# Banded attention in eight larger units: four row groups of score matmuls instead of two, one set of score banks, late projections in banks 6 and 7

## The reference

```python
q = (x @ Wq.T).reshape(b, t, h, e) / scale
kk = (xp @ Wk.T).reshape(b, tp, h, e) / scale      # xp: 31 zero rows ahead of x
v = (xp @ Wv.T).reshape(b, tp, h, e)
idx = jnp.arange(t)[:, None] + jnp.arange(k)[None, :]
dot = jnp.einsum('bthe,btkhe->bthk', q, kk[:, idx])
out = jnp.einsum('bthk,btkhe->bthe', softmax(dot), v[:, idx])
return out.reshape(b, t, h * e) @ Wu.T + bu
```

## Time and profile before

| | us |
|---|---|
| median of 3 runs | 705.16 |
| runs | 700.53 to 710.09 |
| the profiled execution, its own time | 708.41 |
| its span | 706.8 |
| banded attention in it, first warming matmul to end of the last output | 398.6 to 507.5 |

### The profile page before, as it was taken

How to read it: one execution, slowest core, us unless ns; L and a number is a source line. 1 busy time by engine, 2 the same in 40 slices (tenths; PEclk the granted TensorE clock), 3 DMA queues, 4 the chain that set the end, 5 groups by cost and what they waited for, 6 DMA issues and landing times.

```text
span 706.8 us, 8340 instructions
## 1 busy us (share of the span) xinstructions
PE 460.1 (65%) x2996; PEld 244.9 (35%) x3018; DVE 498.6 (71%) x675; ACT 202.4 (29%) x234; POOL 351.3 (50%) x309
## 2 busy tenths in 40 slices
PE   6754845166676667668678878999679953544650
PEld 2531313022222222223223446766446622431210
DVE  1947985889999999999973266677345458976421
ACT  2553791033333323333314332111110052102110
POOL 6617217879999999999960034555730000000000
PEclk8857976569999999999999999687769986757775
DMA  7430020645554545555500000000000000000000
GB/s 273 83 166 1 8 75 2 149 118 151 151 150 149 149 149 149 149 149 149 149 1 8 4 1 2 1 2 3 10 9 1 1 0 0 1 1 7 5 4 32
DMA packets 29262, 46.13 MB, mean 65 GB/s; under 512 B 17878, under 2 KB 19320, under 8 KB 28184
## 3 DMA queue, kind: packets, MB, share of 16 engines
q1 hardware_dynamic: 26776, 45.10, 22.2%
q0 software_dynamic: 2368, 0.37, 0.4%
q10 hardware_dynamic: 64, 0.00, 0.0%
HBM read 43.55 MB, written 1.11 MB: 63 GB/s over the span
## 4 chain that ended last, share of the span: by engine, by line
POOL 30%; PE 21%; DVE 20%; issue 18%; SPq 4%; ACT 4%; DMA 2%; DVEq 1%; POOLq 0%; ACTq 0%
POOL dBu L871 13%; POOL hit L858 9%; SPq L650 3%; PE ps L2185 2%; POOL work L918 2%; PE ps L1867 2%; PE ps L2174 2%; POOL work L920 2%; POOL work L907 2%; PE ps L2077 2%; DMA work<-in_L_attn_edge_index 1%; POOL hst L620 1%; PE ps L2107 1%; PE ps L2321 1%; PE ps L1921 1%
## 5 line engine op out<-in xcount | busy, mean ns | idle before, releaser
L2005 PE MATMUL ps<-hC,ident 128*128 128x512 f32 x256 | 121.4, 596 | 0.0
L1089 ACT ACTIVATE ps<-work,a_neg 128x1020 f32<-128x1020 f32 x64 | 71.3, 1115 | 164.5 <-DVE hst L1429 98.8
L1429 DVE TENSOR_TENSOR_SCAN hst<-ps,dBu 128x1024 f32<-128x1024 f32 x43 | 98.2, 2287 | 4.1 <-ACT ps L1089 1.3
L1989 PE MATMUL ps<-late,pick_state 96*128 96x512 bf16 x128 | 39.5, 391 | 84.2 <-DVE hC L1447 67.9
L871 POOL TENSOR_TENSOR dBu<-work,dA 128x1024 f32<-128x1024 f32 x32 | 75.6, 2361 | 2.8 <-DVE hst L1429 2.2
L871 POOL TENSOR_TENSOR dBu<-work,b_sb 128x1024 f32<-128x1024 f32 x32 | 75.9, 2373 | 0.6
L858 POOL DMA_INDIRECT hit<-in_L_attn_edge_values,tab_i x64 | 63.3, 990 | 12.8 <-issue 10.2
L2005 PEld LDWEIGHTS ps<-hC,ident 128*128 128x128 f32 x256 | 49.1, 192 | 43.1 <-issue 34.1
L1989 PEld LDWEIGHTS ps<-late,pick_state 96*128 96x128 bf16 x128 | 7.8, 97 | 135.2 <-DVE hC L1447 116.9
L1802 PE MATMUL ps<-idle_bf,zero_bf 128*128 128x512 bf16 x133 | 39.4, 431 | 20.2 <-issue 16.5
L1447 DVE TENSOR_TENSOR hC<-hst,ps 128x1024 f32<-128x1024 f32 x43 | 51.4, 1196 | 0.8 <-PE ps L1989 0.8
(11 more groups left out here) (358 smaller groups left out, 876.7 us busy)
## 6 DMA issues: line engine op xcount, KB each, us to landing
b_sb<-b_rows_all SPq DMA_DIRECT2D x64, 256.0 KB, 4.1
dA<-b_rows_all SPq DMA_DIRECT2D x64, 256.0 KB, 4.2
work<-in_L_attn_edge_index SPq DMA_DIRECT2D x6, 1024.0 KB, 6.2
dA<-in_L_attn_edge_index SPq DMA_DIRECT2D x1, 1024.0 KB, 10.6
dBu<-in_L_attn_edge_index SPq DMA_DIRECT2D x1, 1024.0 KB, 12.6
hit<-in_L_attn_edge_values,tab_i POOLq DMA_INDIRECT x64, 3.9
late<-work SPq DMA_DIRECT2D x12, 64.0 KB, 2.0
X<-in_x SPq DMA_DIRECT2D x1, 512.0 KB, 3.9
```

Of the source, the lines that this page charges most:

```text
L1089: nc.scalar.activation(dst[:, :, 1:], src[:, :, 1:], ACT.Exp, scale=a_neg[:, n:n + 1]).then_inc(dA_sb, 1)
L1429: V.tensor_tensor_scan(h_buf[i % 3], dA_ps[k], dBu[:, k, :], 0.0, ALU.mult, ALU.add).then_inc(scan_done, 1)
L1989: last = T.matmul(bank(2 + h), pick_state[:, n, :, :].rearrange("p v i -> p (v i)"), parts[:, j * NT + h * HALF:j * NT + (h + 1) * HALF], ...
L2005: last = T.matmul(bank(6 + h), ident[:, :], hC[:, i % 2, h * HALF:(h + 1) * HALF], start=False, stop=(n == S - 1))
```

## The change

The 16 units become 8: a unit is four heads and one block `j` of all four groups, so every instruction of VectorE, ScalarE and GpSimd in steps 2 to 5 handles 1,024 elements a partition instead of 512, and its buffers grow to match. `unit_scores` has 32 matmuls round four row groups, into banks 0 to 3, one for each group. There is one set of score banks, so it waits for the merge of unit u-1. The warming is one matmul for each of the four banks. `unit_values` and `window_values` come twice in a unit, for groups 0, 1 and 2, 3, through the same banks 4 and 5; the first pair's transpositions stand between the merge and the maximum. `unit_output` goes round four column groups. Projections 3 to 7 use banks 6 and 7; 4 to 7 stand in units 0 and 1, two each, every one waiting for the copy of the one before. The clearing of banks 6 and 7 moves to unit 2. ScalarE's copy of the next unit's scores moves behind the exponential.

In the rows below `[waits ...]` names the semaphores of an instruction. First TensorE in the middle of the loop, one unit of before: the scores of a unit (L2107), values (L2121), the output of an earlier unit (L2134).

The diff, cut where it only changes sizes:

```diff
-        s2_buf = [work[:, 8 * NT + k * HALF:8 * NT + (k + 1) * HALF] for k in range(3)]
+        s2_buf = [area(8 + k, 1) for k in range(3)]
...
+        UNITS = 2 * J
+        SEGS = G * WT
...
-        QM_BANK = (0, 2, 4, 0) + (4,) * 4
+        QM_BANK = (0, 2, 4, 6) + (6,) * 4
...
             def window_keys(u):
...
                 nc.scalar.activation(s2_buf[u % 3].rearrange("p (s k) -> p s k", k=C),
-                                     bank(2 * (u % 2), 2).rearrange("p (s w k) -> p s w k", w=2, k=C)[:, :, 1, :],
+                                     bank(0, 4).rearrange("p (s w k) -> p s w k", w=2, k=C)[:, :, 1, :],
                                      ACT.Copy).then_inc(s2_copied, 1)
...
-            for u in range(16):
-                if u < 15:
-                    window_keys(u + 1)
+            for u in range(UNITS):
+                if u < 2:
+                    query_heads(4 + 2 * u)
                 act.wait_ge(s2_shifted, u + 1)
                 nc.scalar.activation(s2_buf[u % 3], s2_buf[u % 3], ACT.Exp).then_inc(s2_exp, 1)
-                if u < 4:
-                    query_heads(4 + u)
+                if u < UNITS - 1:
+                    window_keys(u + 1)
+                if u < 2:
+                    query_heads(5 + 2 * u)
...
-            def window_values(u):
-                dve.wait_ge(v2_ps, u + 1)
-                if u >= 4:
+            def window_values(u, pair):
+                dve.wait_ge(v2_ps, 2 * u + pair + 1)
+                if u >= 4 and pair == 0:
                     dve.wait_ge(o2_ps, u - 3)
...
-            for u in range(18):
-                if u < 16:
-                    window_scores(u)
-                if 1 <= u < 17:
+            for u in range(UNITS + 2):
+                if u < UNITS:
+                    window_merge(u)
+                    window_values(u, 0)
+                    window_shift(u)
+                if 1 <= u <= UNITS:
                     window_sums(u - 1)
                 if u >= 2:
                     window_probs(u - 2)
-                if u < 16:
-                    window_values(u)
+                if u < UNITS:
+                    window_values(u, 1)
...
-            for h in range(3):
+            for h in range(4):
                 project(h)
-            pe.wait_ge(qm_sb, 1)
-            project(3)
...
             def unit_scores(u):
-                hg, j, gp = unit(u)
-                if u < 2:
+                hg, j = unit(u)
+                if u == 0:
                     pe.wait_ge(qm_sb, 4)
                 else:
-                    pe.wait_ge(s2_read, u - 1)
...
-                for d in range(2):
-                    keep_warm(2, 2 * (u % 2) + d)
+                    pe.wait_ge(s2_read, u)
+                for g in range(G):
+                    keep_warm(1, g)
                 for m in range(WT):
-                    for d in range(2):
-                        g = 2 * gp + d
+                    for g in range(G):
                         r = slice(C * g, C * g + C)
-                        last = T.matmul(bank(2 * (u % 2) + d)[:, 2 * C * m:2 * C * m + 2 * C],
+                        last = T.matmul(bank(g)[:, 2 * C * m:2 * C * m + 2 * C],
...
             unit_scores(0)
-            unit_values(0)
-            for u in range(16):
-                if u < 15:
+            unit_values(0, 0)
+            for u in range(UNITS):
+                if u < 2:
+                    pe.wait_ge(qm_sb, 4 + 2 * u)
+                    project(4 + 2 * u)
+                unit_values(u, 1)
+                if u < UNITS - 1:
                     unit_scores(u + 1)
-                if u < 4:
-                    pe.wait_ge(v2_sb, u + 1)
-                    project(4 + u)
-                if u < 15:
-                    unit_values(u + 1)
+                if u < 2:
+                    pe.wait_ge(qm_sb, 5 + 2 * u)
+                    project(5 + 2 * u)
+                if u == 2:
+                    clear_outputs()
                 if u >= 3:
                     unit_output(u - 3)
-            for u in range(13, 16):
+                if u < UNITS - 1:
+                    unit_values(u + 1, 0)
+            for u in range(UNITS - 3, UNITS):
                 unit_output(u)
```

More of the change, by code:

```diff
@@ L162, in hybrid_kernel @@
         qm = area(0, 8).rearrange("p (t h q) -> p t h q", h=H2, q=C)
-        s2_buf = [work[:, 8 * NT + k * HALF:8 * NT + (k + 1) * HALF] for k in range(3)]
-        pt_buf = [work[:, 8 * NT + (3 + k) * HALF:8 * NT + (4 + k) * HALF] for k in range(2)]
-        lu_buf = [work[:, 11 * NT + k * NT:11 * NT + (k + 1) * NT].rearrange("p (g m w q) -> p g m w q", g=2, m=WT, w=2)
-                  for k in range(2)]
-        vm_buf = [work[:, 13 * NT + k * HALF:13 * NT + (k + 1) * HALF] for k in range(4)]
+        s2_buf = [area(8 + k, 1) for k in range(3)]
+        pt_buf = [area(11 + k, 1) for k in range(2)]
+        lu_buf = [area(13 + 2 * k, 2).rearrange("p (g m w q) -> p g m w q", g=G, m=WT, w=2) for k in range(2)]
+        vm_buf = [area(19 + k, 1) for k in range(4)]
         PAD = C + N
         xpad = work[:, 17 * NT:17 * NT + J * PAD].rearrange("p (j t) -> p j t", t=PAD)
-        mx2 = sb("mx2", [P, 2, 16])
-        sm2 = sb("sm2", [P, 2, 16])
+        UNITS = 2 * J
+        SEGS = G * WT
+        mx2 = sb("mx2", [P, 2, SEGS])
+        sm2 = sb("sm2", [P, 2, SEGS])
         E2 = 8
@@ L927, in _ @@
                     window_bands(u - 1)
-            window_bands(15)
+            window_bands(UNITS - 1)
             pool.wait_ge(gathered, 16 * 2 * C)
@@ L1538, in window_probs @@
                 V.transpose(pt_buf[u % 2], s2_buf[u % 3]).then_inc(p2_t, 1)
-            def window_values(u):
-                dve.wait_ge(v2_ps, u + 1)
-                if u >= 4:
+            def window_values(u, pair):
+                dve.wait_ge(v2_ps, 2 * u + pair + 1)
+                if u >= 4 and pair == 0:
                     dve.wait_ge(o2_ps, u - 3)
-                for g in range(2):
-                    last = V.transpose(vm_buf[u % 4][:, g * N:(g + 1) * N], bank(4 + g)[:, 0:N])
+                for d in range(2):
+                    g = 2 * pair + d
+                    last = V.transpose(vm_buf[u % 4][:, g * N:(g + 1) * N], bank(4 + d)[:, 0:N])
                 last.then_inc(v2_sb, 1)
-            for u in range(18):
-                if u < 16:
-                    window_scores(u)
-                if 1 <= u < 17:
+            for u in range(UNITS + 2):
[4 more added lines that the diff above has]
+                if 1 <= u <= UNITS:
                     window_sums(u - 1)
@@ L2110, in unit_scores, with unit_values @@
                 last.then_inc(s2_ps, 1)
-            def unit_values(u):
-                hg, j, gp = unit(u)
-                if u >= 1:
-                    pe.wait_ge(v2_sb, u)
-                if u <= 4:
-                    pe.wait_ge(qm_sb, 3 if u == 0 else 4 + u)
+            def unit_values(u, pair):
+                hg, j = unit(u)
+                if u + pair > 0:
+                    pe.wait_ge(v2_sb, 2 * u + pair)
                 for d in range(2):
-                    g = 2 * gp + d
+                    g = 2 * pair + d
                     r = slice(C * g, C * g + C)
```

50 lines of the change are left out of this document (25 added, 25 removed).

## The result

The changed kernel takes 687.34 us (median of 4 runs, 686.04 to 687.87); the kernel before, run beside it, 706.01 (4 runs, 700.53 to 710.09). The ratio is 0.9744 with a 95% interval of 0.970 to 0.979. The forecast was 689, range 682 to 702. The number is right, in part by luck: a gain that no term of the sum held and two terms that were wrong pull it in opposite directions, as the experiments show.

A forecast was written before the change was run, and what follows sets the result against it. TensorE was taken to set the pace of most units in the banded attention. The stage's terms ended at 491.15 against 507.48, 16.3 us less: 708.4 to 692.1, less 3.25 for the runs' median, 689 us; range 682 to 702.

The forecast's parts named there:

- Score blocks: TensorE's scores: four row groups run side by side, 64 records in 2.00 us at full clock, 3.68 at 1.2 GHz.
- rival D: Score matmuls: row groups run only as two pairs, blocks take 4.0 us (7.4 at 1.2 GHz), total 713; 7%.
- First merge and units 0 to 2: Start of banded attention: first merge at 402.65, then units of 6.8, 8.5 and 8.7 us, with late projections on the path.
- Units 3 to 6: 4 x 9.7: Middle units, merge to merge: 38.8 us, between 9.15 at full clock and 10.1 at 1.2 GHz, both levels in turn.
- VectorE's row: VectorE's work from merge to merge, with its waits for GpSimd and for ScalarE's copy: 9.15 us a unit.
- The copy's releaser: ScalarE's copy of the next unit's scores is released by VectorE's transposition, because there are three score buffers, instead of by scores.
- Two other signs of being right: Middle of the stage: merges 9 to 10 us apart and VectorE 85% busy.
- GpSimd and the drain: GpSimd takes 6.5 us a unit; unit 7 and the drain, paced by GpSimd, take 25.7 us.
- Rival B: Clock stays at 2.4 GHz: units 3 to 6 at 9.15, tail 25.3, 18.9 us less, total 686; 15%.
- Rival E: Clock low throughout the stage because TensorE idles: stage ends at 508.7, 1.2 us more, total 706; 9%.
- Nothing changes after it: Behind the banded attention: no change in time, so the whole gain is the stage's 16.3 us.
- The runs' median, 705.16, lies 3.25 below that execution, so the forecast is 688.9: Whole kernel: 692.1 us on the profiled execution, lowered by the gap between runs' median and that execution, rounded to 689.

The follow-up runs named there:

- e2: Changed kernel with each unit's score matmuls in two blocks, row groups 0 and 1, then 2 and 3; 704.27 us, ratio 0.993 to 1.002.
- e3: Changed kernel with six and eight more idle matmuls on zeros a unit in TensorE's waits, from units 2 and 3 on; 684.51 us.
- e4: Changed kernel without the four warming matmuls ahead of the scores of units 4 to 7; 683.76 us.
- e6: Changed kernel with the last unit's scaling and two band products on VectorE instead of GpSimd; 684.14 us.
- e11: e10 with the scaling of unit 7 and the bands of units 6 and 7 on VectorE instead of GpSimd; 676.66 us.
- e9: Changed kernel with 64 filler instructions on VectorE behind the stage's last transposition, so later code stands where it stood before; 695.52 us.
- e1: The kernel before, unchanged, profiled a second time; 704.71 us (one run).
- e7: e4 with a fourth buffer for the scores, so ScalarE's copy no longer waits for the transposition three units back; 683.08 us.
- e10: e4 with VectorE's sum of the unit before put between the maximum and the subtraction; 680.67 us.
- e13: e11 with the fourth score buffer of e7; 675.64 us.
- e12: e11 with all warmings back and the further idle matmuls of e3 added; 677.63 us.
- e5: The kernel before with one warming matmul instead of two ahead of each half of a unit's scores; 723.76 us.

## Why the prediction was right, and where it was not

**Score blocks: right.** 2.01 and 3.69 us for 64 records, forecast 2.00 and 3.68. e2 shows what the rival D would have cost: 17 us, not the 24 priced, since its blocks took 3.4 and 6.3 us and not 4.0 and 7.4. The output was right too: 64 records take 1.05 us at full clock (e3), forecast 1.04.

**First merge and units 0 to 2: right.** From first warming to first merge 4.11 us (forecast 4.06), then 6.74, 8.56, 8.38 (6.8, 8.5, 8.7).

**"Units 3 to 6: 4 x 9.7": the term that was mis-sized.** They took 9.81 + 3 x 10.46 = 41.2, not 38.8. Three errors. First, I took both clock levels in turn; in fact the clock fell once and stayed down. Second, the low-clock path was put at 10.1, with 1.4 for warmings from a row of three records; four take 1.81. Third, that path was drawn through the merge. In the trace it goes through the output (1.75 us), which stands between the scores and the first values and had no term; the 0.7 for late first values stood in for it and was nearly its size (merge to first transposition 1.84 us, forecast 2.0). VectorE's row was sized well: 8.94 in e3 against 9.15. Its reciprocal took 0.35 where I put 0.2, its wait for GpSimd 0.85 where I put 0.8.

**The copy's releaser: wrong in this kernel, right beneath it.** I expected VectorE's transposition; the scores released it seven times of eight. With TensorE's path shortened (e3) or its late warmings gone (e4) the transposition does. Two other signs of being right did not come: merges 10.46 apart instead of 9 to 10, and VectorE busy for 31.2 of the 41 us from 426 on, 76% and not 85%.

**GpSimd and the drain: right.** 6.35 us a unit (6.5), tail 25.24 (25.7), paced by GpSimd; e6 and e11 shorten it by taking work from GpSimd.

**Rival B and the clock.** The Trainium skill, "TensorE: Matmul & The Clock Gate", section "HAM oscillation — how this bites in real kernels", asks for long idle gaps before the clock drops. The trace of the changed kernel differs: it dropped after gaps of 1.5 us at most. The prediction followed the row and not the page on whether the clock would fall, and that held. Rival E had the clock right for five of eight units and the price wrong, since units 0 to 2 ran at full clock.

**The stage as a whole:** warming to last output 94.2 us, forecast 92.6: 2.4 more in units 3 to 6, 0.8 less in units 0 to 2 and the drain.

**"Nothing changes after it" failed.** 8.2 us of the change's gain come with the place of VectorE's code (e9), in a part of the program that the change does not touch.

**"The runs' median, 705.16, lies 3.25 below that execution, so the forecast is 688.9" failed as well.** The difference lay in the very stage that the change replaces: it took 108.9 us in that execution and 103.4 in e1's, while the changed stage took the same time in e9 as in the changed kernel. It should not have been taken off again; that is argued from two profiles of the kernel before, not shown by a run of its own. Without this, the forecast is 692.1; with 1.6 us more for the stage it is 693.7, and e9, the changed kernel with the code where it was, has 695.5. The 8.2 us unseen pull one way and the 3.25 taken off wrongly and the mis-sized units the other, on the way to 687.3. So the mechanism in the stage was forecast rightly but for the loop of units 3 to 6, and that the total came within 2 us of 689 is luck. The attention change alone brings the time to 0.982 to 0.990 of what it was, about 10 us, not 18.7, and would not have passed the prediction's 2% line of 691.

## What to carry to other kernels

Compare a change with a control that keeps the code behind it where it was: filler instructions in a place where the engine waits anyway tell what belongs to the change. A median that lies below the profiled execution may be subtracted only where the changed part is not itself the cause. Where two waits stand in series on one engine, remove the later one before judging the earlier one (alone the fourth buffer gave nothing in e7; behind e10's order, in e13, it brought some merges to 7.7 to 7.9 us, until TensorE's loop was the bound). Filler work that keeps the clock up can itself become the bound (e12). And where two engines exclude one another, order the work so that their two-operand instructions miss each other.

## What was unexpected of the hardware

A taken branch on VectorE cost 2.8 to 3.5 us or 0.3 us by where the code stood, the largest single finding (8.2 us with all that came with it). The granted clock stayed at 1.2 GHz for 71.7 us in which TensorE was busy for 51.0 of 71 us, and fell with no gap over 1.5 us in the 20 us ahead; in e3, with TensorE busy 36.6 of 41 us, it stayed at 2.4 GHz. The busy time alone does not tell the two apart: in the 41 us from 426 on TensorE was busy for 36.9 us in the changed kernel too. In the kernel before, taking 32 warmings of a quarter microsecond away cost 18 us (e5), in the changed one taking 16 away gained 3.6 (e4). Four row groups, with 64 columns to a matmul, did twice the work of two in the same time: 64 records in 2.01 us, 32 in 2.00. What decides when the clock falls stays open: no run here isolates it. Which of VectorE's code borders moved was not tried either.
